# Staged value blocks: the writers' blocks stored ahead of four held-back gathers, values alone staged, patches apart, expert loads earlier in the queue

## The reference

```python
x = x + einsum('bct,bcd->bdt', x, W0[cond])                # layer 0: gathered mixing of tokens
x = x + x @ W1.T + lora(x, A[adapter], Bm[adapter], s)     # layer 1: LoRA per sequence
x = x + paged_attention(x, ...)                            # layer 2
x = x + x @ W3[expert] + b3[expert]                        # layer 3: one expert per sequence
```

```python
blk = take_along_axis(block_tables, pos // 16, axis=1)
k_blocks = k_blocks.at[blk, :, pos % 16, :].set(k); v_blocks likewise
k_all = k_blocks[block_tables]; v_all = v_blocks[block_tables]
allowed = (kpos <= pos) & (kpos > pos - 128)
p = softmax(where(allowed, q @ k_all.T * SCALE, -inf));  o = p @ v_all;  out = o @ Wo.T
```

## Time and profile before

| | |
|---|---|
| median of 3 executions | 156.03 us (155.38 to 156.3) |
| the profiled execution | 154.9 us, of which the span from first to last instruction 153.1 us |
| PE busy | 117.3 us (77%) |
| DVE, ACT, POOL busy | 88.8, 85.8, 62.0 us |
| chain that ended last | DMA 42%, PE 20%, SP's queue 17%, issue 9% |
| largest lines of the chain | `kv_rows<-blkp` 15%, `wr_rows<-blkp` 11% |

### The profile page before, as it was taken

One profiled execution on the slowest core, in us unless ns is written; L12 is line 12 of the kernel. 1 busy time (PEld: TensorE's weight loads), 2 busy tenths in 40 slices (PEclk: granted clock), 3 DMA queues, 4 the chain that ended last, 5 costly groups with the idle time before them and its releaser, 6 DMA issues.

```text
span 153.1 us, 4138 instructions
## 1 busy us (share of the span) xinstructions
PE 117.3 (77%) x1418; PEld 91.0 (59%) x1418; DVE 88.8 (58%) x315; ACT 85.8 (56%) x236; POOL 62.0 (41%) x65
## 2 busy tenths in 40 slices
PE   7569599999989586076598392892599999999762
PEld 7559458998374163074466272672387787776631
DVE  0597988857528824860344003610867999989361
ACT  3119634698743629256589721472438878888200
POOL 7666779000008764787233300330333444734000
PEclk9999999999999977659969758699569999999999
DMA  3982999999963444799739998999976676766110
GB/s 94 244 249 62 370 424 407 423 405 374 395 173 100 132 119 114 247 313 392 315 110 269 422 355 210 401 377 279 253 232 205 197 242 204 222 207 180 37 39 34
DMA packets 29100, 37.60 MB, mean 246 GB/s; under 512 B 9497, under 2 KB 26781, under 8 KB 27438
## 3 DMA queue, kind: packets, MB, share of 16 engines
q1 hardware_dynamic: 26136, 23.98, 50.0%
q0 software_dynamic: 2528, 12.82, 22.2%
q10 hardware_dynamic: 416, 0.56, 1.2%
HBM read 31.39 MB, written 10.04 MB: 271 GB/s over the span
## 4 chain that ended last, share of the span: by engine, by line
DMA 42%; PE 20%; SPq 17%; issue 9%; POOL 5%; DVE 3%; ACT 2%; POOLq 1%; DVEq 0%
DMA kv_rows<-blkp 15%; DMA wr_rows<-blkp 11%; PE bank L1117 5%; DMA blkp<-wr_rows,patch_i 4%; PE bank L1063 4%; POOL wr_rows L500 4%; DMA blkp<-in_L_cond_W 4%; PE bank L1075 3%; PE bank L1128 3%; SPq L386 3%; DMA mask_rows<-span_m 3%; DMA scal<-in_L_cond_scalings 3%; SPq L364 2%; SPq L365 2%; SPq L348 2%
## 5 line engine op out<-in xcount | busy, mean ns | idle before, releaser
L520 POOL TENSOR_TENSOR xin_m<-xin_m,ri 128x704 f32<-128x704 f32 x15 | 21.8, 1454 | 44.4 <-DVE ri L924 44.4
L674 ACT ACTIVATE xin_m<-kvn_m,nb 128x176 f32<-128x176 f32 x64 | 27.6, 443 | 9.2 <-DVE nb L911 9.2
L911 DVE CUSTOM_DVE_ANT_0 kvn_m<-bank,mask_m 128x176 f32<-128x176 f32 x64 | 18.0, 336 | 14.6 <-PE bank L1063 11.0
L951 DVE TENSOR_TENSOR blkp<-blkp,cst 128x512 f32<-128x512 f32 x16 | 15.6, 1015 | 17.6 <-DMA blkp<-in_L_cond_W 17.6
L1063 PE MATMUL bank<-kt_m,natQ 32*64 32x176 f32 x256 | 15.7, 366 | 10.0 <-DVE nb L911 9.1
L1063 PEld LDWEIGHTS bank<-kt_m,natQ 32*64 32x64 f32 x256 | 9.5, 150 | 14.2 <-issue 13.1
L500 POOL DMA_INDIRECT wr_rows<-kvn_m,row_i x8 | 8.8, 1104 | 21.3 <-DMA wr_rows<-blkp 19.1
L684 ACT COPY x_m<-bank 128x512 f32<-128x512 f32 x16 | 9.4, 590 | 13.0 <-PE bank L1075 12.8
L1043 PE MATMUL bank<-cst,blkp 121*128 121x121 f32 (+1 forms) x48 | 9.0, 352 | 7.8 <-DMA blkp<-wr_rows,patch_i 7.8
L1043 PEld LDWEIGHTS bank<-cst,blkp 121*128 121x128 f32 (+1 forms) x48 | 7.3, 190 | 10.0 <-DMA blkp<-wr_rows,patch_i 9.0
L674 ACT ACTIVATION_READ_ACCUMULATOR xin_m<-kvn_m,nb 128x1 f32 x64 | 12.8, 200 | 0.0
(11 more groups left out here) (194 smaller groups left out, 257.4 us busy)
## 6 DMA issues: line engine op xcount, KB each, us to landing
blkp<-in_L_cond_W SPq DMA_DIRECT2D x32, 256.0 KB, 3.5
kv_rows<-blkp SPq DMA_DIRECT2D x3, 2048.0 KB, 10.3
wr_rows<-blkp SPq DMA_DIRECT2D x1, 1536.0 KB, 16.5
mask_m<-mask_rows SPq DMA_DIRECT2D x32, 44.0 KB, 5.4
vm_m<-kv_rows SPq DMA_DIRECT2D x4, 320.0 KB, 4.4
xin_m<-in_x SPq DMA_DIRECT2D x2, 512.0 KB, 5.6
out<-wq_m SPq DMA_DIRECT2D x8, 128.0 KB, 3.5
vm_m<-kv_rows SPq DMA_DIRECT2D x2, 384.0 KB, 4.6
```

The costliest lines, as they stand in the source:

```text
L520: pool.tensor_tensor(e_, e_, ri[:, p % 2, :].unsqueeze(2).broadcast_to([P, 4, KEYS]), ALU.mult).then_inc(s_pn, 1)
L674: act.activation(pr_seq(n % 2, u, j), S[:, n % 2, u, j, :], ACT.Exp, bias=nb[:, n % 2, 2 * u + j:2 * u + j + 1], scale=-1.0, accum_out=rs[ ...
L911: dve.tensor_tensor_reduce(S[:, n % 2, u, j, :], bank[2 + (2 * n + u) % 3][:, j * KEYS:(j + 1) * KEYS], mask[:, 2 * n + j, :], -SCALE, 3e3 ...
L951: tt(w_, w_, ident.unsqueeze(1).broadcast_to([P, B4, P]), ALU.add).then_inc(s_wx, 1)
```

## The change

- SP: the eight mask loads that stood before the writers' store now stand behind it. Sixteen masks follow the store, and the other sixteen are spread: four after `values_out(0)`, four after `values_out(1)`, eight after `values_out(2)`, each time ahead of the `values_back` of the same unit. DVE waits for masks in four groups of eight.
- POOL: the gathers of units 1 and 2 are held until both permutes of the writers' blocks are done.
- `values_out` stores only the values of the blocks that are used, in pieces of 512 bytes (121 x 16 or 110 x 16 of them), to a new tensor `v_rows`; before, it stored keys and values of 128 partitions in rows of 16 KB.
- `patch(2)` waits for `values_out(0)` to land.
- `expert(0..3)` stands ahead of `values_out(1)` and `expert(4..7)` ahead of `values_out(2)`; experts 8 to 15 use `blkp[1]` in place of `blkp[2]`.
- The four permutes of units 1 and 2 are all on DVE (before: one there, three on ACT). The last two query norms (`q_part[2]`, `q_part[3]`) move from before the loop into steps 0 to 5 of DVE's loop (`Q_STEP`), with the turns of their queries and of eight key pieces at later steps. The bias gathers stand one to a step in POOL's loop.

```diff
@@ values and masks on SP
-            for b in range(8):
-                load_mask(b)
             for kv in range(2):
                 sp.wait_ge(s_perm[NU, kv], 1)
             sp.dma_start(wr_blocks, blkw[0:NWI, :]).then_inc(s_base, 16)
-            for b in range(8, B):
+            for b in range(2 * MB):
                 load_mask(b)
...
             def values_out(u):
                 sp.wait_ge(s_patch[u], 16)
-                sp.dma_start(kv_rows[u], blkp[u][:, :]).then_inc(s_vo[u], 16)
+                sp.dma_start(v_rows[u, 0:PU[u]], by_o[u][0:PU[u], :, 1, :]).then_inc(s_vo[u], 16)
...
             values_out(0)
+            for b in range(2 * MB, 2 * MB + 4):
+                load_mask(b)
             values_back(0)
-            values_out(1)
             for b in range(4):
                 expert(b)
+            values_out(1)
+            for b in range(2 * MB + 4, 3 * MB):
+                load_mask(b)
             values_back(1)
-            values_out(2)
             for b in range(4, 8):
                 expert(b)
+            values_out(2)
+            for b in range(3 * MB, B):
+                load_mask(b)
             values_back(2)
@@ POOL
-            for i in ((NU, 0), (NU, 1), (0, 0), (0, 1), (1, 0), (1, 1)):
+            for i in ((NU, 0), (NU, 1), (0, 0), (0, 1)):
                 load_blocks(i)
...
+            for kv in range(2):
+                pool.wait_ge(s_perm[NU, kv], 1)
+            load_blocks((1, 0))
+            load_blocks((1, 1))
             pool.wait_ge(s_l0, 4)
             load_blocks((2, 0))
...
+            patch(0)
+            patch(1)
+
+            pool.wait_ge(s_vo[0], 16)
+            patch(2)
...
+                n = p - BIAS_STEP
+                if 0 <= n < NT:
+
+                    pool.indirect_dma_start(out=be[n], out_offset=None, in_=b3,
@@ DVE
-            permute((2, 0))
+            for i in ((1, 0), (1, 1), (2, 0), (2, 1)):
+                permute(i)
             dve.wait_ge(s_rt, 8)
-            for i in range(4):
+            for i in range(2):
                 for piece in q_part[i]:
                     piece()
+            for i in range(2, 4):
+                q_part[i][0]()
...
                     if n == 0:
-                        dve.wait_ge(s_mask, 16 * B)
                         dve.wait_ge(s_new, 16 * NT)
+                    if n % (MB // 2) == 0:
+                        dve.wait_ge(s_mask[2 * n // MB], 16 * MB)
...
+                if n in Q_STEP:
+                    i, piece = Q_STEP[n]
+                    q_part[i][piece]()
@@ steps
-        QT_STEP = {1: 4, 2: 5, 3: 6, 4: 7}
-        KT_STEP = {0: (6, 7), 1: (8, 9), 2: (10,), 3: (11,)}
+        QT_STEP = {3: 4, 4: 5, 6: 6, 7: 7}
+        KT_STEP = {0: (4, 5), 1: (6, 7), 2: (8, 9), 3: (10, 11)}
+        Q_STEP = {0: (2, 1), 1: (2, 2), 2: (2, 3), 3: (3, 1), 4: (3, 2), 5: (3, 3)}
+        BIAS_STEP = 2
```

More of the change, by code:

```diff
@@ L47 @@
 NE = 16
+MB = 8
 LAST = WINDOW + BLOCK - 2
@@ L285, in program @@
             "k_sums_ready", "k_roots_ready", "q_sums_ready", "q_roots_ready", "norm_step", "k_ready", "q_ready"))
-        s_span, s_spanm, s_spanw, s_shift, s_mask = (sem(n) for n in (
-            "span_squared", "span_mask_ready", "span_mask_written", "shifts_ready", "masks_loaded"))
+        s_span, s_spanm, s_spanw, s_shift = (sem(n) for n in (
+            "span_squared", "span_mask_ready", "span_mask_written", "shifts_ready"))
+        s_mask = [sem(f"masks_loaded{i}") for i in range(B // MB)]
         s_vz = sem("v_tails_zeroed")
@@ L296, in program @@
         s_wx = sem("residual_added")
-        s_be = [sem(f"expert_bias_loaded{i}") for i in range(2)]
+        s_be = [sem(f"expert_bias_loaded{i}") for i in range(NT)]
         s_out = [sem(f"output_written{i}") for i in range(2)]
@@ L364, in load_mask @@
                 x = sp.value_load(shift_i[0:1, b:b + 1], min_val=0, max_val=LAST)
-                sp.dma_start(mask[:, b, :], mask_rows[:, bass.ds(x, KEYS)]).then_inc(s_mask, 16)
-            for b in range(8):
-                load_mask(b)
+                sp.dma_start(mask[:, b, :], mask_rows[:, bass.ds(x, KEYS)]).then_inc(s_mask[b // MB], 16)
             for kv in range(2):
@@ L504, in _, with patch @@
             pool.wait_ge(s_pidx, 1)
-            for u in range(NU):
+            def patch(u):
                 for kv in range(2):
@@ L632, in _ @@
             root_k(1)
-            permute((1, 0))
             keep_v(1)
@@ L643, in _ @@
             root_q(1)
-            permute((2, 1))
+            act.wait_ge(s_perm[2, 1], 1)
+            act.activation(vt_m[:, 0:RAW], ones[:, 0:1].broadcast_to([P, RAW]), ACT.Copy, scale=0.0).then_inc(s_vz, 1)
             keep_x2(2)
@@ L647, in _ @@
             keep_qn(2)
-            act.wait_ge(s_perm[2, 1], 1)
-            act.activation(vt_m[:, 0:RAW], ones[:, 0:1].broadcast_to([P, RAW]), ACT.Copy, scale=0.0).then_inc(s_vz, 1)
-            root_q(2)
             keep_qn(3)
-            root_q(3)
-            act.activation(warm[:, 1:2], eps[:, 0:1], ACT.Exp)
-            for c in range(6):
+            for c in range(4):
                 if c == 0:
@@ L659, in _ @@
                 keep_kt(c)
[L660 to L664, removed]
+            for t in range(4):
+                keep_qt(t, bank[QT_BANK[t // 2]][:, t % 2 * D:t % 2 * D + D])
+            root_q(2)
+            root_q(3)
+            act.activation(warm[:, 1:2], eps[:, 0:1], ACT.Exp)
             for n in range(PAIRS + TURN):
@@ L676, in _ @@
                                            accum_out=rs[:, n % 2, 2 * u + j:2 * u + j + 1]).then_inc(s_exp, 1)
-                for c in KT_STEP.get(n, ()):
-                    keep_kt(c)
+                if n in KT_STEP:
+                    keep_kt(KT_STEP[n][0])
                 p = n - TURN
@@ L1048, in scores @@
                     pe.wait_ge(s_qk, 8)
[L1049 to L1053, removed]
+                pe.wait_ge(s_ktk, 4 * (UNIT_OF[2 * p + 1] + 1))
                 if p % 4 == 0:
@@ L1204, in _ @@
             pe.wait_ge(s_x2, 4)
-            for t in range(2):
-                turn_q(t, bank[QT_BANK[0]][:, t * D:t * D + D])
-            for c in range(4, 6):
-                turn_k(c)
-            for t in range(2):
-                turn_q(2 + t, bank[QT_BANK[1]][:, t * D:t * D + D])
+            for t in range(4):
+                turn_q(t, bank[QT_BANK[t // 2]][:, t % 2 * D:t % 2 * D + D])
             scores(0)
@@ L1214, in _ @@
                     scores(n + 1)
-                for c in KT_STEP.get(n, ()):
-                    turn_k(c)
+                if n in KT_STEP:
+                    turn_k(KT_STEP[n][0])
                 g = group_at(n, PROJECT)
@@ L1225, in _ @@
                     layer3(g)
+                if n in KT_STEP:
+                    turn_k(KT_STEP[n][1])
             pv(PAIRS - 2)
```

33 lines of the change are left out of this document (16 added, 17 removed).

## The result

The changed kernel takes 162.41 us (median of 3, 160.76 to 163.11) against 156.03. The ratio is 1.040 [1.026, 1.053], so it is 4% slower where 3.4% faster was forecast. A second measurement gave 162.09 us and 1.037 [1.029, 1.044]. Some executions are over 1.5% longer than the shortest of the same kernel in the same measurement, and the medians here leave these out. The profiled execution has a span of 160.6 us against 153.1.

A forecast was written before the change was run, and what follows sets the result against it. A chain of waits (writers' store, scatters, patch, values stores, expert loads) bounds the kernel until n = 7. Its release at 108.3 against 113.63 gains 5.3 us: 154.9 - 5.3 = 149.6, plus 1.1 for the median, 150.7 us; range 146 to 157.

The forecast's parts named there:

- Step 1, the writers' store: Writers' store on SP, issued at 25.5 us with no masks ahead, lands at 33.4, 11.5 us sooner.
- Step 2, scatters and first patch: POOL's scatters start at 34.3 us, the last lands at 47.0; first patch lands at 54.5 against 65.82.
- an edit that I had costed at nothing: Four permutes on DVE: delay to PE's query projection and first scores stays hidden, even up to 7 us.
- Step 3, the chain of stores: SP's values stores, reads, experts and masks after the first patch: stores 9.5, 8.5, 8.5 us; n = 7 released at 108.3.
- 6 are given back: experts in series: On SP, experts 0 to 7 in series with stores and last masks give back 6 of 11.3 us won.
- The rival of fewer engines: Values stores of 121 and 110 rows run on 11 of 16 engines, 1.6 us more each: 155.5 us; chance 0.17.
- The rival of the mask loads in the way: SP can't push masks until the store's pieces are gone; n = 7 at 116.6, time 159 us; chance 0.15.
- The rival of faster issue: With smaller stores SP issues all expert loads at 1.04 us each, 4 us less: 146.7 us; chance 0.15.
- The rival of the gathers: Held-back gathers ahead in POOL's queue hold the scatters, 3 us more: 153.7 us; chance 0.05.
- What would show it: Trace signs: store near 33 us, first patch 54 to 55, DVE waits shrinking at n = 3 and 5, growing at 7.

## Why the prediction was wrong, by its own steps

- **Step 1, the writers' store: right.** Forecast 33.4, landed at 34.7. Its blocks came 1 us late from ACT (26.4 for 25.46).
- **Step 2, scatters and first patch: right in part, 5.4 us short** (59.92 for 54.5). I had the first scatter go when the store lands (34.3). It went at 37.87, since it waited for DVE's normed keys (L888). These stand behind `row_i` in DVE's order, and the 2.58 us of idle before `row_i` aren't the program's. From there the eight scatters followed each other on POOL. Some 2.4 us were the two scatters beside DVE's copies, an edit that I had costed at nothing: I looked for its cost at PE's scores and not at POOL's issues. The rest is a patch of 7.12 for 6.73.
- **Step 3, the chain of stores: its structure right, its sizes wrong.** From the patch's landing to n = 7 I had 53.8 us; it took 60.1. The terms: the first store to its reads 9.5, as forecast, but for another reason, since it had landed and the masks held SP. Its reads 4.7 for 2.1. The second store 10.5 for 8.5 and its reads 3.3 for 2.1. The third 13.0 for 8.5. Experts and gaps took 4.1 less than forecast.
- **The step that failed** is the middle of step 3, by which a mask costs SP 1.03 us and fits inside a landing, and a store runs on all 16 engines and is read after 8.5 us. The runs showed in its place 1.7 us for each of four masks and 1.3 for each of eight, and stores on 11 engines that were read after 9.5, 10.5 and 13.0 us. The row for the masks, 1.03, was taken where no store stood ahead. The better row stood beside it: 24 masks behind the writers' store at 1.29. With both terms mended (128 rows, masks where SP waits) n = 7 came at 108.9, and at 110.2 on the chip with the wait at `row_i`, for the 108.3 of the forecast.
- **"6 are given back: experts in series"** was no loss: undoing it gained nothing.
- **The rival of fewer engines** (0.17) was true, and its price came out, 4.8 us forecast and 5.3 measured; in part by luck, since the stores themselves gave 3.5 of it and the reads behind them, which it didn't name, 2.8.
- **The rival of the mask loads in the way** (0.15) was the one case that forecast slower, and its mechanism was true: n = 7 was 5.2 us sooner without them. But masks moved alone left 1.031, and it was the 128 rows that brought the time back to 1.004. I had priced each beside an otherwise right forecast, and never added them: 150.7 + 4.8 + 8.3 is 163.8, for 162.4 measured.
- **The rival of faster issue** (0.15) was true of the experts, for another reason than small stores. Experts 0 to 3 and 4 to 7 took 3.81 and 3.82 us, 0.95 each, for the 6.0 and 6.5 of the sum. With 16 KB rows in the stores they took 3.81 and 3.80, so it is their place ahead of the stores that made them fast. The masks and reads behind the stores swallowed the gain. The 4.3 us to a store beside it is an estimate from figures that the Trainium skill (DMA: Bandwidth & Descriptors, Anatomy of one DMA) gives for DMAs issued from GpSimd. The values stores are SP's, and in no run was one read sooner than 7.1 us after its issue, so the figures don't price them.
- **The rival of the gathers** (0.05) didn't show in the changed kernel, whose last scatter landed in 2.42 us. Where the scatters came sooner it can't be left out (4.07 and 5.26 us). None of my cases had DVE's copies in POOL's way.
- **What would show it.** Waits shrinking at n = 3 and growing at n = 7 came true. At n = 5 the wait grew. Of the three signs of being wrong, a first patch after 58, stores over 10 us and n = 7 after 113, all came.

What stays open: what DVE's `row_i` waits for in some executions, what holds a scatter that is issued before 46 us, and why one mask or one read behind a store holds SP for up to 3 us. That the queue is full then is argued from the rows, not shown by a run of its own.

## What to carry to other kernels

Before a store is cut to the rows that matter, look at how many rows are left: here 121 and 110 rows cost 5 us against 128, and made the cut store slower than the whole one. A DMA issued behind a store isn't priced by a row where no store stood ahead, and what stands between a store and its read-back is on the chain; put it where the queue waits for something else. And where two rivals work on different terms of one sum, price them together.

## What the runs showed of the hardware

- A store whose source has 121 rows keeps the DMA engines busy for 68.3% of the time of all 16, which is 11 of them, and one of 128 rows for 92.2%; a piece of 512 bytes to DRAM takes 0.030 and 0.026 us, about as it does from DRAM, 0.029.
- Behind such a store a mask load takes 1.3 to 1.7 us of SP instead of 1.03 (1.25 to 1.4 behind a store of 16 KB rows), and an expert load 1.8 to 2.7 (four in 7.08 and in 10.61 us) instead of 0.95 to 1.3.
- A float32 copy on DVE stretches the issue of an indirect DMA on POOL from 1.0 us to as much as 2.4.
